# An exponential in place of a tangent in the router of an attention and mixture-of-experts kernel

## The reference

```python
z = jnp.einsum('btd,ed->bte', x, proj_w)          # 6 numbers a token
q = jnp.tanh(z / QUANT_TEMP)                      # QUANT_TEMP = 0.3
dot = jnp.einsum('btd,ed->bte', q, anchors)       # anchors: 6 x 6, of -1 and 1
hamming = (6.0 - dot) * 0.5
logits = -hamming / jnp.clip(routing_temp, 0.1)
topk_logits, topk_idx = jax.lax.top_k(logits, TOP_K)
topk_w = jax.nn.softmax(topk_logits, axis=-1)
```

## Time and profile before

| | |
|---|---|
| median of 3 runs | 670.87 us (669.88 to 672.49) |
| profiled execution | 669.76 us |
| its span | 668.0 us |
| granted TensorE clock, mean | 0.948 of full speed |
| busy: PE, DVE, ACT, POOL | 598.8, 414.5, 355.4, 301.4 us |
| attention stage with its setup | until about 350 us of the span |
| blocks 0 to 4 are squashed at | 189, 232, 276, 318 and 348 us |

### The profile page before, as it was taken

How to read it: one execution, slowest core, us unless ns; L and a number is a source line. 1 busy time by engine, 2 the same in 40 slices (tenths; PEclk the granted TensorE clock), 3 DMA queues, 4 the chain that set the end, 5 groups by cost and what they waited for, 6 DMA issues and landing times.

```text
span 668.0 us, 14302 instructions
## 1 busy us (share of the span) xinstructions
PE 598.8 (90%) x4512; PEld 448.9 (67%) x4512; DVE 414.5 (62%) x880; ACT 355.4 (53%) x674; POOL 301.4 (45%) x434
## 2 busy tenths in 40 slices
PE   5789999999999999988897899998999999989950
PEld 3665566666666656654455689897999999978740
DVE  4765766566577567662787945467873346665653
ACT  3636865676584736736768446352344554444420
POOL 4523765646355555456676613224000045645534
PEclk9968999999998979979997799999999999999985
DMA  5411222122212235617365536568576779999986
GB/s 159 128 43 38 80 79 88 58 95 96 96 48 88 91 110 166 213 63 253 128 217 178 220 112 222 188 206 330 172 229 229 224 252 351 394 405 404 382 288 189
DMA packets 60275, 122.09 MB, mean 183 GB/s; under 512 B 7718, under 2 KB 10790, under 8 KB 60204
## 3 DMA queue, kind: packets, MB, share of 16 engines
q1 hardware_dynamic: 49964, 87.61, 39.2%
q0 software_dynamic: 10240, 33.56, 14.0%
HBM read 67.93 MB, written 53.22 MB: 181 GB/s over the span
## 4 chain that ended last, share of the span: by engine, by line
PE 60%; issue 10%; DVE 9%; DMA 9%; POOL 5%; ACT 3%; SPq 3%; POOLq 0%; DVEq 0%; ACTq 0%
PE ps L1482 8%; DMA y_d<-ysb 6%; PE ps L1504 5%; PE ps L1647 4%; PE ps L1527 4%; PE ps L1529 3%; PE ps L1528 3%; PE ps L1702 3%; PE ps L1704 3%; PE ps L1703 3%; PE ps L1728 3%; PE ps L1730 3%; PE ps L1729 3%; PE ps L1688 3%; PE ps L1602 3%
## 5 line engine op out<-in xcount | busy, mean ns | idle before, releaser
L794 POOL DMA_INDIRECT yg<-y_d,y_row x64 | 65.0, 1015 | 129.3 <-DMA y_d<-ysb 73.1
L909 ACT ACTIVATE prob<-ps 128x512 f32<-128x512 f32 x128 | 66.1, 602 | 86.7 <-PE ps L1507 84.0
L1082 DVE TENSOR_REDUCE nmax<-ps 128x4 f32<-128x512 f32 x128 | 82.0, 685 | 46.6 <-PE ps L1482 46.4
L723 POOL DMA_INDIRECT xs_d<-x,to_row x64 | 68.4, 1068 | 71.9 <-DVE to_row L1147 35.5
L1702 PE MATMUL ps<-w1H,xgH 128*128 x276 | 83.7, 303 | 5.0 <-issue 2.7
L1482 PEld LDWEIGHTS ps<-kfT,qT 32*128 32x128 f32 x1024 | 69.9, 200 | 21.0 <-issue 17.9
L1367 DVE TENSOR_TENSOR xgL<-ps,xgH 128x512 fp32r<-128x512 f32 x69 | 47.5, 688 | 55.6 <-ACT xgH L990 51.2
L1482 PE MATMUL ps<-kfT,qT 32*128 32x128 f32 x1024 | 77.3, 292 | 3.6 <-DVE nmax L1082 2.6
L1704 PE MATMUL ps<-w1L,xgH 128*128 x276 | 77.8, 282 | 0.0
L1703 PE MATMUL ps<-w1H,xgL 128*128 x276 | 77.6, 281 | 0.0
L1728 PE MATMUL ps<-w2H,hH 128*128 x138 | 60.3, 437 | 1.1 <-DVE ysb L1380 1.0
(11 more groups left out here) (212 smaller groups left out, 1329.2 us busy)
## 6 DMA issues: line engine op xcount, KB each, us to landing
xg<-xs_d SPq DMA_DIRECT2D x69, 256.0 KB
y_d<-ysb SPq DMA_DIRECT2D x69, 256.0 KB
xin<-in_x SPq DMA_DIRECT2D x32, 256.0 KB, 2.7
x<-in_x SPq DMA_DIRECT2D x32, 256.0 KB
x_d<-x SPq DMA_DIRECT2D x32, 256.0 KB
x2t<-x_d SPq DMA_DIRECT2D x32, 256.0 KB
out_x<-x2t SPq DMA_DIRECT2D x32, 256.0 KB
w1L<-in_L_ffn_w SPq DMA_DIRECT2D x6, 512.0 KB, 8.2
```

The source lines that it names most:

```text
L723: nc.gpsimd.indirect_dma_start(xs_d, bass.IndirectOffsetOnAxis(ap=to_row[:, n, k, t:t + 1], axis=0), x2[:, n % 4, t, :], None).then_inc(sc ...
L794: nc.gpsimd.indirect_dma_start(yg[:, c % RY, z, :], None, y_d[0:TILES_OF[c // 4] * P, :], bass.IndirectOffsetOnAxis(ap=y_row[:, c, z:z + 1 ...
L909: nc.scalar.activation(prob[v % 2][:, h, :], ps[:, B_SC + h, :], ACT.Exp, scale=scale).then_inc(exp_done, 1)
L1082: nc.vector.tensor_reduce(nmax[:, n % 2, :, g * hpg + h], ps[:, token_bank(v, h), :].rearrange("p (t k) -> p t k", t=4), axis=AX.X, op=ALU ...
```

## The change

For blocks 0 to 4 squash no longer takes the Tanh of z/0.3 but the Exp of 2z/0.3, and no table set is named afterwards. router_logits then forms the tangent from it in place, as 1 - 2/(e + 1), with three VectorE instructions on the 128x24 tile qr, each waiting for the one before: an addition, a reciprocal, and a multiplication with an addition. Blocks 5 to 7 keep the Tanh.

```diff
--- before.py
+++ after.py
@@ -342,6 +342,7 @@
         nmr2_done, zp_ready, zp_done = sem("nmr2_done"), sem("zp_ready"), sem("zp_done")
         t2_ready, t2_done = sem("t2_ready"), sem("t2_done")
         x2_out = sems("x2_out", 2)
+        th = sem("th")
         z_ready, q_done, rt, qa_done, ldif_done, lexp_done, wsel_done, slot_done, w_done = (
             sem("z_ready"), sem("q_done"), sem("rt"), sem("qa_done"), sem("ldif_done"), sem("lexp_done"), sem("wsel_done"),
             sem("slot_done"), sem("w_done"))
@@ -889,10 +890,8 @@
                 if live(n, nblk):
                     act.wait_ge(z_ready, n + 1)
                     after(act, qa_done, n)
-                    nc.scalar.activation(qr[:], ps[:, z_bank(n), 0:4 * 6].rearrange("p (t d) -> p t d", t=4), ACT.Tanh,
-                                         scale=1.0 / QUANT_TEMP).then_inc(q_done, 1)
-                    if n + 2 < INSIDE:
-                        nc.scalar.preload_act_table_set("natural_log_exp_and_others")
+                    nc.scalar.activation(qr[:], ps[:, z_bank(n), 0:4 * 6].rearrange("p (t d) -> p t d", t=4), ACT.Exp if n + 2 < INSIDE else ACT.Tanh,
+                                         scale=(2.0 if n + 2 < INSIDE else 1.0) / QUANT_TEMP).then_inc(q_done, 1)
 
             def exponentials(n):
                 if live(n, nblk):
@@ -1085,12 +1084,23 @@
 
             RT = 7
 
+            def tanh(n):
+
+                def link(ins, k):
+                    ins.then_inc(th, 1)
+                    dve.wait_ge(th, 3 * n + k)
+                link(nc.vector.tensor_scalar(qr[:], qr[:], 1.0, None, ALU.add), 1)
+                link(nc.vector.reciprocal(qr[:], qr[:]), 2)
+                link(nc.vector.tensor_scalar(qr[:], qr[:], -2.0, 1.0, ALU.mult, ALU.add), 3)
+
             def router_logits(n):
                 def link(ins, k):
                     ins.then_inc(rt, 1)
                     dve.wait_ge(rt, RT * n + k)
                 dve.wait_ge(q_done, n + 1)
-
+                if n + 2 < INSIDE:
+
+                    tanh(n)
                 nc.vector.tensor_tensor(qa[:], qr[:].unsqueeze(2).to_broadcast([P, 4, EXPERTS, 6]),
                                         anc[:].unsqueeze(1).to_broadcast([P, 4, EXPERTS, 6]), ALU.mult).then_inc(qa_done, 1)
                 dve.wait_ge(qa_done, n + 1)
```

## The result

The changed kernel takes 672.59 us in the median of 20 runs, the kernel before 670.12 in 20 runs; the ratio is 1.0053, with a 95% interval of 1.0031 to 1.0075. The ratios and, further down, the means of the clock are formed from fast executions alone. This ratio is 3.5 us more (2.1 to 5.0); the plain medians are 2.5 us apart. I had forecast 671.2, that is 0.35 us above before. The sign is as forecast and the measured time lies inside the range that I gave, but the cost is seven to ten times the forecast one, and the chance that I gave to "slower by more than 0.5%" was 0.12, where the ratio now stands just at that line.

What follows compares the result with a forecast made beforehand. The chain that ended last bound the kernel, TensorE 60% of it, ScalarE 3%. Terms + 2.0 (blocks 0 to 2), - 0.45 (block 3), - 1.2 (block 4) gave + 0.35 us on 670.87: median 671.2, range 667.6 to 674.0.

Steps and rivals of the forecast that it cites:

- The sign: Whole kernel: slower, by 0.35 us, to a median of 671.2 us.
- slower by more than 0.5%: Whole kernel: a measured time above the 3.35 us band around no change, which reaches to 674.2 us; chance 0.12.
- The loads are hidden in blocks 0 to 2: Squash, blocks 0 to 2: ScalarE waits for TensorE anyway, so removing two table loads a block gains 0.
- my sum: Whole kernel: + 2.0 (blocks 0 to 2) - 0.45 (block 3) - 1.2 (block 4) = + 0.35 us.
- VectorE's chain: Router, blocks 0 to 2: three new instructions make sel, which TensorE awaits, later; 2.0 us in all, bounds 0 and 5.8.
- two collisions: Router: VectorE waits out GpSimd's second large operation, at gt or over in block 0 and at ldif in block 1.
- Block 3 and block 4: Removed loads gain 0.45 us at TensorE's scores in block 3 and 1.2 us at copy x2T in block 4, capped by sel.
- The clock: TensorE's granted clock behind its waits: no term in the forecast's sum; a change in it was left to rivals.
- Rival (a): Blocks 0 to 2: longer waits bring more lower clock, 677 us, or 672.7 with block 0's full stretch alone; chance 0.10.

## Why the prediction was right and where it was not

**The loads are hidden in blocks 0 to 2: right.** L908 now waits 3.18 us in block 0 and about as long in the two others (I had said more than 3), and the kernel without the loads and without the instructions is level with before until the step ahead of block 3's squash. There the 0.3 us are lost that my sum had put at nothing; this is the one thing that the loads' removal did to the chain and that I hadn't seen.

**VectorE's chain: right in its mechanism, 0.36 us small in its size.** I took 2.0 us and 2.36 came; the waits rose by 0.85, 0.78 and 0.76 us, to 2.30, 2.29 and 2.22, which I had put at 1.9 to 2.4. What I had wrong in size were two collisions. In block 0 gt was caught as I had counted, but L775 took 1.44 us, not 1.26, and gt ended 0.16 behind it. In block 1 GpSimd's second operation started 0.12 us sooner behind its first than before, and so it caught lgs, not ldif; from a caught lgs to the end of sel it is 1.54 us, in place of the 1.11 that I had from ldif:

```profile
239.54 1.27 POOL L775 TENSOR_TENSOR atL<-atT,atH 128x512 fp32r<-128x512 f32 x1 [0.84 <-POOL atT L767]
239.66 1.19 DVE L1109 TENSOR_SCALAR lgs<-dot,tinv 128x24 f32<-128x24 f32 x1
```

The reciprocal, too, is longer than the row that I had it from, 0.30 us on 128x24 against 0.18, but that costs nothing in these blocks: the instruction behind it is caught by L767 and ends with it, 1.01 to 1.02 us long in each of the three, as said. The Trainium skill, "SBUF — State Buffer", section "Who interferes with whom", says that whichever of the two engines issues first holds the port pair for its whole instruction. The trace agrees: the same tensor_scalar takes 1.02 us beside L767 and 0.18 us where the three instructions were moved away from GpSimd's big operations.

**Block 3 and block 4: right.** I had 0.45 and 1.2; the residuals show 0.49 and 1.05. sel became what is late next in block 4, behind an ldif caught by L775, as worked out. TensorE's two waits there, for x2T and for sel, are 2.88 us together after the change and 1.77 without the VectorE instructions, against 4.02 before, which shows that the chain to sel is what capped the gain.

**The clock: the step that failed.** My sum had no term for it. I put a longer wait's effect on the granted clock into a rival with a chance of 0.10, on the ground that the 4.02 us of block 4 were followed by a slow stretch hardly longer than that behind 1.5 us. One long wait says little about what follows, since block 0 (3 us slow) and block 1 (7 us slow) already differed behind equal waits in the same profile. What the timed runs hold above the change's own items is 3.5 - 1.1 = 2.4 us (1.0 to 3.9 by the interval, 1.3 by the plain medians); the clocks of the kernels with the same waits give 1.3 to 2.3 us as an estimate. So the term that I had put at nothing is about as large as the cost of the chain. Rival (a) has the right mechanism. That its price for one stretch more in block 0, 672.7, is the measured time is partly luck: in the profile block 0's stretch stayed as long as it was, block 1's grew, and the expert stage added time of its own.

**What is not settled.** It is open why ScalarE starts x2T 0.28 us later ahead of block 3's squash step in every kernel whose blocks 0 to 2 lost their loads, how the clock's part grows with the length of the wait, and why the expert stage differs from profile to profile by more than the change. In the profiles the setup moves a kernel by 0.3 to 3.1 us, either way, before the first edited block.

## What to carry to other kernels

An engine that is 53% busy gives nothing back for work taken from it unless the chain passes it: look, place by place, at what its next instruction waited for. Put small linked instructions where their engine waits anyway, and not between a result and the engine that stands waiting for it, and away from GpSimd's large operations. A wait of TensorE is dearer than its length: here taking 1.1 us off each of three waits brought 8 to 10 us, by ratio and by medians in two sessions.

## What the runs showed of the hardware

The reciprocal of 128x24 took 0.30 us where a tensor_scalar of that shape took 0.15 to 0.18; on 128x4 a reciprocal took 0.18. TensorE's granted clock stood at 0.5, the level of 1.2 GHz, behind waits of only 1.5 us between stretches of full work, and could stay there for 13 us of unbroken matmuls (block 1, after); with waits of 0.4 us or less it never fell between 190 and 300 us in five profiles. Equal waits were answered differently from run to run, and this, with 661.9 to 676.9 us for one and the same kernel before, is why a change of two microseconds in the chain needs many runs to be seen.
